# Two convolution layers merged into one instruction block, the next image pair's input work woven into each attention's end

## What is computed

```python
attn = jnp.einsum('bhnd,bhmd->bhnm', q * scale, k)
rel_h = jnp.einsum('bnhwc,hkc->bnhwk', rq, Rh)
rel_w = jnp.einsum('bnhwc,wkc->bnhwk', rq, Rw)
attn = (attn.reshape(Bw, NH, WS, WS, WS, WS) + rel_h[..., :, None] + rel_w[..., None, :]).reshape(Bw, NH, N, N)
attn = jax.nn.softmax(attn, axis=-1)
out = jnp.einsum('bhnm,bhmd->bhnd', attn, v)
```

## Time and profile before

| | us |
|---|---|
| median of 3 runs | 1480.7 (1478.15 to 1488.42) |
| the profiled execution, its own time | 1474.58 |
| its span, first to last instruction | 1472.4 |
| mean granted TensorE clock | 0.829 of 2.4 GHz |
| TensorE busy over the span | 1127.6 |
| VectorE, ScalarE, GpSimd busy | 581.0, 390.0, 88.9 |
| start of L0's first projection stage | 27.44 |
| end of L1's last projection product | 539.43 |

### The profile page before, as it was taken

The page is one execution under the profiler, slowest core; times in us unless marked ns, Lnnn a source line. Parts: engine busy times, 40 slices in busy tenths (PEclk is TensorE's granted clock), DMA queues, the critical chain, the costliest instruction groups (busy, mean ns, idle before and its releaser), DMA issues. The chain is left out here.

```text
span 1472.4 us, 27845 instructions
## 1 busy us (share of the span) xinstructions
PE 1127.6 (77%) x10374; PEld 781.0 (53%) x10375; DVE 581.0 (39%) x1709; ACT 390.0 (26%) x932; POOL 88.9 (6%) x130
## 2 busy tenths in 40 slices
PE   2779796976687779897968519994697897558993
PEld 1647464843554547574736407773373573436772
DVE  5143112323232527473857612222573374421223
ACT  2103210320141145352524103331251252112220
POOL 2000010000000000000000040003100000040004
PEclk9769785977697799897979659997797998768997
DMA  7000000002000000007400141111920000021113
GB/s 190 3 2 3 1 2 2 3 1 83 4 1 1 3 1 1 1 2 160 162 0 1 33 110 43 48 48 46 206 74 1 0 2 1 1 72 46 48 48 102
DMA packets 32150, 57.28 MB, mean 39 GB/s; under 512 B 3557, under 2 KB 28870, under 8 KB 31018
## 3 DMA queue, kind: packets, MB, share of 16 engines
q1 hardware_dynamic: 28856, 48.44, 12.2%
q0 software_dynamic: 3072, 6.30, 1.5%
q10 hardware_dynamic: 114, 1.04, 0.3%
HBM read 41.80 MB, written 13.86 MB: 38 GB/s over the span
## 5 line engine op out<-in xcount | busy, mean ns | idle before, releaser
L1612 PE MATMUL banks<-gu,sxT 96*128 x496 | 177.8, 503 | 0.8 <-ACT sxT L1647 0.6
L215 PE MATMUL banks<-xT,weights 96*96 96x512 f32 (+3 forms) x288 | 148.5, 675 | 9.4 <-ACT xT L423 8.8
L1013 ACT ACTIVATE work<-banks,nmax 128x128 f32<-128x128 f32 (+1 forms) x288 | 105.6, 418 | 108.0 <-DVE nmax L1052 107.8
L1673 DVE TENSOR_TENSOR h<-sg,banks 128x384 f32<-128x384 f32 x62 | 34.4, 554 | 236.4 <-ACT sg L1655 236.4
L1612 PEld LDWEIGHTS banks<-gu,sxT 96*128 96x128 f32 x496 | 92.7, 197 | 54.6 <-issue 7.6
L1052 DVE TENSOR_REDUCE nmax<-banks 128x2 f32<-128x256 f32 (+1 forms) x144 | 80.2, 557 | 64.4 <-PE banks L957 62.3
L215 PEld LDWEIGHTS banks<-xT,weights 96*96 96x96 f32 (+3 forms) x288 | 55.1, 196 | 92.7 <-issue 73.9
L932 PE MATMUL banks<-K,Q 96*128 96x128 f32 (+1 forms) x384 | 86.1, 351 | 11.1 <-PEq L88 11.1
L696 ACT ACTIVATE work<-banks 98x1024 f32<-98x1024 f32 (+1 forms) x48 | 49.2, 1024 | 144.8 <-PE banks L620 144.8
L754 DVE TENSOR_REDUCE nmax<-banks 98x4 f32<-98x784 f32 (+1 forms) x48 | 52.6, 1100 | 74.7 <-PE banks L594 54.2
L1061 DVE COPY work<-banks 128x256 f32<-128x256 f32 (+1 forms) x144 | 79.2, 550 | 0.4
(11 more groups left out here) (235 smaller groups left out, 1661.4 us busy)
## 6 DMA issues: line engine op xcount, KB each, us to landing
gu<-in_L2f_gu SPq DMA_DIRECT2D x1, 6912.0 KB, 37.0
xin<-slots_in SPq DMA_DIRECT2D x62, 96.0 KB, 1.9
slots_out<-y SPq DMA_DIRECT2D x62, 96.0 KB
gu<-in_L3f_gu SPq DMA_DIRECT2D x1, 5184.0 KB, 31.4
dn<-in_L2f_dn SPq DMA_DIRECT2D x1, 4608.0 KB, 47.9
slots_in<-zeros SPq DMA_DIRECT2D x1, 2976.0 KB, 10.8
dn<-in_L3f_dn SPq DMA_DIRECT2D x1, 2592.0 KB, 37.3
gu<-in_L2f_gu SPq DMA_DIRECT2D x1, 2304.0 KB, 13.0
```

The lines of the kernel that those rows point to most:

```text
L215: ins = nc.tensor.matmul(out, lhs(k, rows), rhs(k, rows), start=(k == 0), stop=(k == 1))
L1013: ins = nc.scalar.activation(w.Pr[0:rows, s % 3, hh, 0:lay.width(t)], S(s)[0:rows, hh, 0:lay.width(t)], ACT.Exp, bias=w.nmax[0:rows, s % 4 ...
L1612: ins = nc.tensor.matmul(banks[:, 2 + 2 * par + n, 0:EF], w.sxT[:, par, k, :], w.gu[:, bass.ds(e, 1), k, n * EF:(n + 1) * EF].rearrange("p ...
```

## The change

The stages of both layers, eleven with L1's setup, become one block, `convolution_layers`, in which the instructions of attention, next input and feed-forward are written in one order for each engine. The classes `Relative` (one object for each layer) and `PlainFeedForward` hold the steps as methods; their arithmetic is that of before. What differs:

- Scores of the first image (`u` 0 to 5) are placed between the relative products (`late`): product group `g`, then scores `g - 1`. They use banks 3 to 6, and the slivers' maxima there take two VectorE reductions for each unit instead of one.
- `main` then alternates scores 6 to 11 with turned scores 0 to 5.
- In the loop over (layer, pair, next layer, next pair) the input turning, statistics, both queries and key group 0 of the next pair stand between turned scores 6 to 11. The last `weigh`, the turning of the outputs, `turn_normed` and `project` of the second image come before key groups 1 to 5 and the values. For L0 the feed-forward comes after those values, and before the next `late`.
- Turned scores always use banks 4 and 5, also at the end.
- The residual is added in `X` itself; the copies through `R` are gone. The feed-forward has an input buffer of its own (`fxT`). L1's tables are made in the attention of L0's pair 0 and spread in that of pair 1. GpSimd's window copies no longer wait for each other.
- ScalarE loads Exp at the start, and Gelu and Exp again around each feed-forward.
- The DMA of zeros into `slots_in` (needed much later) moves from L1's setup to L0's.

```diff
-def relative_setup(nc, env, w, windows):
+def relative_setup(nc, env, w, w1):
...
+    def s_banks(self, u):
+        if u < 6:
+            return (4, 5), (6, 3)
+        return ((0, 1), (2, 3)) if self.windows or u % 2 == 0 else ((2, 3), None)
...
+    def pe_scores_turned(self, pe, ip, u):
+        nc, w, ck = self.nc, self.w, self.ck
+        m, g = divmod(u, 6)
+        q, k = w.Q[:, g, m * TOKENS:(m + 1) * TOKENS], w.K[:, g, m, :]
+        pe.wait_ge(self.max_in[u // 3], 32 * (ip + 1))
+        if u == 0:
+            pe.wait_ge(self.max_ready, self.parts * (12 * ip + 6))
+        else:
+            pe.wait_ge(self.exp_ready, 12 * ip + u)
...
+    def pe_turn_outputs(self, pe, ip, m, t):
+        nc, w = self.nc, self.w
+        pe.wait_ge(self.O_out, 6 * ip + 3 * m + 3)
+        if (m, t) == (0, 0):
+            pe.wait_ge(self.NT_out, 4 * ip + 4)
+        elif (m, t) == (0, 1):
+            pe.wait_ge(self.normed, 4 * ip + 1)
+        elif (m, t) == (1, 0):
+            pe.wait_ge(self.added, PAIR * ip + 1)
...
+            def late(L, ip, ring_read=None):
+                for g in range(6):
+                    L.pe_relative(pe, ip, g, ring_read)
+                    if g >= 1:
+                        L.pe_scores(pe, ip, g - 1)
+                    if g == 4:
+                        L.pe_turn_max(pe, ip, 0)
+                L.pe_scores(pe, ip, 5)
+            def main(L, ip):
+                for i in range(6):
+                    L.pe_scores(pe, ip, 6 + i)
+                    if i in (0, 3):
+                        L.pe_turn_max(pe, ip, 1 + i // 3)
+                    L.pe_scores_turned(pe, ip, i)
+                    if i in (2, 4):
+                        L.pe_weigh(pe, ip, i // 2 - 1)
+            L0.pe_turn(pe, 0)
+            for a in range(2):
+                L0.pe_queries(pe, 0, a)
+            for g in range(6):
+                L0.pe_keys(pe, 0, g)
+            for j in range(L0.jobs):
+                L0.pe_values(pe, 0, j)
+            late(L0, 0)
+            main(L0, 0)
+            for L, ip, N, nip in ((L0, 0, L0, 1), (L0, 1, L1, 0), (L1, 0, L1, 1), (L1, 1, None, 0)):
+                L.pe_turn_max(pe, ip, 3)
+                L.pe_scores_turned(pe, ip, 6)
+                L.pe_weigh(pe, ip, 2)
+                if N is not None:
+                    N.pe_turn(pe, nip)
+                L.pe_scores_turned(pe, ip, 7)
+                L.pe_turn_outputs(pe, ip, 0, 0)
+                if (N, nip) == (L0, 1):
+                    L1.pe_window_tables(pe)
+                L.pe_scores_turned(pe, ip, 8)
+                L.pe_weigh(pe, ip, 3)
+                L.pe_turn_outputs(pe, ip, 0, 1)
+                if N is L1:
+                    N.pe_stats(pe, nip)
+                L.pe_scores_turned(pe, ip, 9)
+                L.pe_turn_normed(pe, ip, 0)
+                L.pe_scores_turned(pe, ip, 10)
+                L.pe_weigh(pe, ip, 4)
+                L.pe_project(pe, ip, 0)
+                if N is not None:
+                    N.pe_queries(pe, nip, 0)
+                L.pe_scores_turned(pe, ip, 11)
+                if N is not None:
+                    N.pe_queries(pe, nip, 1)
+                    N.pe_keys(pe, nip, 0)
+                L.pe_weigh(pe, ip, 5)
+                L.pe_turn_outputs(pe, ip, 1, 0)
+                L.pe_turn_outputs(pe, ip, 1, 1)
+                L.pe_turn_normed(pe, ip, 1)
+                L.pe_project(pe, ip, 1)
+                if N is not None:
+                    for g in range(1, 6):
+                        N.pe_keys(pe, nip, g)
+                    for j in range(N.jobs):
+                        N.pe_values(pe, nip, j)
+                    if L is L0:
+                        F.pe(pe, ip, (N.v_out, N.jobs * (nip + 1)))
+                    late(N, nip, (F.added, PT * (ip + 1)) if L is L0 else None)
+                    main(N, nip)
...
+            def late_and_main(L, ip, extra, per_step):
+                L.dve_relative(dve, ip, 1)
+                L.dve_maxima(dve, ip, 0)
+                L.dve_maxima(dve, ip, 1)
+                L.dve_relative(dve, ip, 3)
+                L.dve_maxima(dve, ip, 2)
+                L.dve_maxima(dve, ip, 3)
+                L.dve_turned_max(dve, ip, 0)
+                L.dve_relative(dve, ip, 5)
+                L.dve_maxima(dve, ip, 4)
+                L.dve_maxima(dve, ip, 5)
+                for i in range(6):
+                    L.dve_maxima(dve, ip, 6 + i)
+                    if i in (0, 3):
+                        L.dve_turned_max(dve, ip, 1 + i // 3)
+                    for _ in range(per_step):
+                        next(extra, None)
+                for _ in extra:
+                    pass
...
+            for L, ip, N, nip in ((L0, 0, L0, 1), (L0, 1, L1, 0), (L1, 0, L1, 1), (L1, 1, None, 0)):
+                L.dve_turned_max(dve, ip, 3)
+                if N is L1:
+                    N.dve_stats(dve, chain, nip)
+                L.dve_divide(dve, chain, ip, 0, 0)
+                if (N, nip) == (L0, 1):
+                    L1.dve_window_tables(dve, chain)
+                L.dve_divide(dve, chain, ip, 0, 1)
+                if N is L1:
+                    N.dve_affine(dve, chain, nip)
+                L.dve_residual(dve, ip, 0)
+                if N is not None:
+                    N.dve_keys(dve, nip, 0)
+                if L is L0:
+                    dve.wait_ge(L.added, PAIR * ip + 1)
+                    for _ in F.norm_steps(chain, ip, 0):
+                        pass
+                L.dve_divide(dve, chain, ip, 1, 0)
+                L.dve_divide(dve, chain, ip, 1, 1)
+                L.dve_residual(dve, ip, 1)
+                if N is not None:
+                    for g in range(1, 6):
+                        N.dve_keys(dve, nip, g)
+                if L is L0:
+                    dve.wait_ge(L.added, PAIR * ip + 2)
+                    for _ in F.norm_steps(chain, ip, 1):
+                        pass
+                    chain.wait()
+                    dve.sem_inc(F.normed, 2)
+                    F.dve_add(dve, ip)
+                if (N, nip) == (L0, 1):
+                    late_and_main(N, nip, window_tables_steps(nc, chain, w1), 2)
+                elif (N, nip) == (L1, 1):
+                    late_and_main(N, nip, input_ahead(0), 5)
+                elif N is not None:
+                    late_and_main(N, nip, iter(()), 0)
...
-                relative_setup(nc, env, w, windows)
-                for ip in range(IMAGES // PAIR):
-                    relative_project(nc, env, w, ip, windows)
-                    attend_relative(nc, env, w, ip, windows)
-                    if windows:
-                        feed_forward(nc, env, w, ip, False)
...
+            relative_setup(nc, env, w, w1)
+            convolution_layers(nc, env, w, w1)
```

1045 lines of the change are left out of this document (560 added, 485 removed).

## The result

| | before | after |
|---|---|---|
| median, us | 1482.5 (1478.2 to 1488.4, 4 runs) | 1431.2 (1422.3 to 1433.6, 4 runs) |
| ratio | | 0.964, 95% interval 0.959 to 0.970 |
| span of the profiled execution, us | 1472.4 | 1429.4 |
| TensorE's granted clock, mean | 0.83 | 0.84 |

The change made the kernel 51 us faster. I had forecast 1391 (1364 to 1427): the direction was right, the size was not, and the time lies above the range.

A forecast was written before the change was run, and what follows sets the result against it. TensorE's stream was taken as the bound, losing to low clock, instruction waits, maxima waits and stage fronts. Savings 16.5 + 7.0 + 18.3 + 18.7 + 8.0 + 11.6 + 8.3 - 1.5 - 0.6 = 86.3 us gave 1388, put at 1391 (1364 to 1427).

The forecast's parts named there:

- Sum 49: Each L0 late stretch, first relative product to turned scores 6: 26 plus 23 us, saving 16.5 and 18.3.
- 40.3 in all: Each L1 late stretch, first relative product to turned scores 6: 40.3 us, saving 8.0 and 8.3.
- 1632 instructions in 20.3 us: L1 late stretch: instruction fetch sets the time of the interleaved relative products and scores, 20.3 of 40.3 us.
- The end of L0 pair 0, 82.9: Turned scores 6 of L0 pair 0 to the next pair's first relative product: 82.9 against 89.9 us, 7.0 saved.
- The new stall of 3.4 us: End of each L0 attention: PE waits 3.4 us for VectorE, late with key copy, image 0's normalisation and divisions.
- The end of L0 pair 1, 76.1: Turned scores 6 of L0 pair 1 to the next first relative product: 76.1 against 94.85 us, 18.7 saved.
- the wait for one bank pair: L0 attention's end: turned scores with little between them wait for their banks, costing 0.6 us.
- Rival (b), the clock stays down: After the new stall until the feed-forward, keys and values double, 19 and 11 us more: 1421 us; chance 0.20.
- The ends of L1, 38.6: End of L1's first pair, with next pair's work woven in: 38.6 against 50.2 us, 11.6 saved; very last end loses 1.5.
- 0.6 lost: Before the first attention: the first relative product now waits for the last value copy, 0.6 us lost.
- Rival (a): TensorE's clock stays up in late stretches and ends, L0 late stretches taking 23.6 + 21.7 us: 1374 us; chance 0.17.
- Rival (c): Fetching isn't overlapped in the relative groups, 1.6 us staying with each packet, about 40 us more: 1431 us; chance 0.06.

The follow-up runs named there:

- No weaving: Changed kernel with the next pair's input, queries and first key group as one block behind each attention's last projection: 1448.9 us, 0.977 of the kernel before.
- no alternation: Changed kernel with all six relative groups first and the six scores behind them in each late stretch: 1459.0 us, 0.983 of the kernel before.
- the second profile: The changed kernel run again without any edit, beside the kernel before on one chip: 1418.8 us, 0.956 of the kernel before.

## Why the prediction was wrong in size

The mechanisms held, and most stretches came out as worked out. Point by point:

- *Which losses go.* Right. The waits for maxima are gone or short, and those on "issue" fell from 7.5 to 3.3 us in the first late stretch. No weaving costs 30 us, no alternation 40.
- *"Sum 49" and "40.3 in all", the late stretches.* **This is the step that failed every time**: 18.8 us over the four, 21.1 in the second profile. Three terms of it were too small. First, the fetch: I let PE at half clock hide it everywhere, but the first two relative groups stand back to back, with no score between, and wait for instructions: 3.3 us in L0 pair 0, 1.1 to 1.6 in the others, with 1.0 more behind a later group of L1 pair 1. With a value job between them that is gone. Second, the relative group: 1.86 us came from taking the weight loads' 8.2 us of waiting off the row of the products, whose own waits are 7.5; with those it is 1.98, and 2.0 to 2.06 were measured, at either clock, about 1 us more in each stretch. Third, L1: I took "1632 instructions in 20.3 us" as the bound and charged 1.2 us for the clock. The stretch up to the first turned scores ran at 0.53, and six groups and six scores at half clock took 24.1, which is 2.6 above the 20.3 and 1.2. The 4.8 us missing in L1 pair 0 are these 2.6, 1.1 of fetch, 0.5 for scores 6 at half clock and 0.5 in the alternating part. I had made the half-clock sum for L0, found it above the fetch, and did not make it for L1. In L0 I also took 26 where my own half-clock sum had 27.2; the part before the alternating units took 30.8. The alternating part took 23.5 against 23.
- *The end of L0 pair 0, 82.9.* 82.7, and 81.0 in the second profile; the 1.7 between them are mostly a short fall of the clock behind turned scores 6, so that 82.7 meets 82.9 partly by luck. The new stall of 3.4 us came as 3.35:

```profile
141.59 0.87 PE L555 MATMUL banks<-small,Os 128*128 128x128 f32 x6 [0.52 <-ACT Os L632]
145.82 1.09 PE L564 MATMUL banks<-small,On 128*96 128x128 f32 x4 [3.35 <-DVE On L765]
147.77 2.61 PE L215 MATMUL banks<-weights,OT 96*128 96x192 f32 x7 [0.86 <-ACT OT L642]
```

- *The end of L0 pair 1, 76.1.* 76.3 in two profiles (in the second of them 322.12 less 245.87), 91.6 and 94.4 (342.59 less 248.16) in the other two, and three of the four times behind the result are at 1431 or more. The step that failed: "the wait for one bank pair: ... with little between them, 0.6". I priced the waits between turned scores 6, 7 and 8 as idle time and did not look at what stands in front of scores 6, where only 0.4 us of turning maxima lie between them and scores 5. The wait is 0.89 us; behind it the clock falls in some executions, and with the wait taken away it falls there in none.
- *Rival (b), the clock stays down.* The nearest to what happened, but it had the fall start behind the new stall and cost keys and values. It began 45 us earlier and cost turned scores and queries; keys 1 to 5 took 9.5 us, near the 8.65 of full clock. The Trainium skill, "TensorE: Matmul & The Clock Gate", section "HAM oscillation — how this bites in real kernels", tells of a kernel whose waits for transfers, 3 to 5 us, throttle the array every time. Here the clock fell behind a wait of 0.89 us, and only in two profiles of four, so the trace agrees in part.
- *The ends of L1, 38.6.* 41.6 and 41.5: behind waits of 0.92 and 0.68 us, priced as idle time, the clock falls; the projection took 2.93 us, where I had 1.5, and the first keys ran at half clock too.
- *The front.* "0.6 lost" was 3.5. The change makes the first query product wait for both halves of its input, which I had not noticed in the diff (0.86 us); most of the rest is the slow pace of the first products, which lasts to between 34.4 and 37.5 us in four profiles, in place of 30.8. Where that wait is taken away it lasts to 36.5, 32.3 and 36.8, so the wait is not its cause, and the cause of the length stays open.
- *Rival (a)* fell: in all profiles of the changed kernel the late stretches run at 0.53 to 0.60. *Rival (c)* gave 1431 by the wrong way: 40 us of fetch waits, of which 8 exist over the four stretches.
- *The range.* It would have held the second profile's 1419. Its upper end came from one rival with one place for the fall of the clock; two misses of the same sign, one certain and one by chance, were not in it.

What stays open: why the clock falls behind the same wait in one execution and not in the next, and why it falls a second time only in some of those.

## What to carry to other kernels

Work out every stretch at half clock as well as by its instructions, layer by layer, and take the larger. Where a wait of under 1 us interrupts small products, look at it as a possible fall of the clock with all that stands behind it: here 0.89 us of idle time stood in front of a loss of 15 us, and two free banks removed both. Compare stretches, and not only whole times, where kernels ran on different chips: the unchanged part of this one took 933 to 942 us. And take a second profile before explaining a stretch: of one kernel's four, two differed from the others by 15 us or more in one place.

## What the runs showed of the hardware

- A relative group (64 products of 32x32, recorded as 128 instructions) takes 2.10 us at granted clock 0.50 and at 1.00. A score unit of L0 takes 2.43 and 1.37, a value job of L0 2.88 and 1.55.
- Relative groups back to back wait for instructions 4.1 to 9.6 us in each stretch of six; with scores between them 1.1 to 3.3 us, with a value job and a score between them not at all.
- The first products after TensorE had stood idle for 28 us run at half pace (weight loads of 96x512 products 0.85 us apart against 0.43). The slow time is 3.4 us in both profiles of the kernel before and 4.3 to 9.8 us in the changed ones. It ends where the trace's first clock record starts; before that record the view shows 1.00. With added products from 12.6 us on, the first products ran at full pace in one profile; in another three of them were slow, at a granted clock of 0.50.
- The granted clock of a stretch is not fixed by the order of instructions: 0.74 and 0.91 for the same 630 products in two executions. Behind the same wait of 0.89 us it fell 11 times of 20.
